# Readers of one PSUM buffer in another order: a decoder layer's cross attention and its FiLM step

## The chip, the cores and the metric

The kernel runs on one core of a Trainium2 chip. A core has five engines with a queue of instructions each: TensorE (PE in the profile: matmuls, and PEld for the loads of their stationary operand), VectorE (DVE), ScalarE (ACT), GpSimd (POOL) and SyncE (SP, which issues DMAs here). They run beside each other and are ordered among each other by semaphores alone. The metric is the device time of one execution in microseconds (us); less is better.

## The reference

The computation is a two-layer decoder on x of 16 sequences x 256 rows x 256 columns, with a context of 77 rows x 192 columns for each sequence. Layer 0 is windowed attention, cross attention and a network of eight experts. Layer 1 is what the change lies in; cut to it, on x after layer 0:

```python
x = x + _L1_attn_ref(_layernorm(x))      # RWKV: a scan over the 16 sequences, then a channel mix
# _L1_xattn_ref(x_text = _layernorm(x), x_vision = ctx_768):
Q, K = x_text @ Wq, x_vision @ Wk                            # 4 heads of 32
topv, topi = jax.lax.top_k(scores, K_TOP)                    # the 32 best of 77 keys
attn_mean = attn.mean(axis=1)                                # mean over the heads
c_t = einsum(attn_mean, x_vision @ Wv)
x = layernorm(x_text, g_norm_in, b_norm_in)
scale_in, shift_in = split(c_t @ W_film_in + b_film_in)
x = x * (1.0 + mod_gate * scale_in) + mod_gate * shift_in    # FiLM before the state space model
y = s4d(x, ...)                                              # a filter, by a Fourier transform
scale_out, shift_out = split(c_t @ W_film_out + b_film_out)
y = y * (1.0 + mod_gate * scale_out) + mod_gate * shift_out  # FiLM behind it
xt = x_text + y
h = layernorm(xt, g_ffn, b_ffn); xt = xt + gelu(h @ W1 + b1) @ W2 + b2
return layernorm(xt, g_norm_out, b_norm_out)
# then x = x + _L1_ffn_ref(_layernorm(x)): a product with a sign matrix, scaled and clipped
```

## The kernel before

The first half of the program (to about 915 us) is layer 0; the change doesn't touch it. The second half is one function, `mixing_and_state_space`, a software pipeline over the 16 sequences. Its loop has 20 steps, n = 0 to 19, and each engine's queue is written out by hand: every engine runs the same loop and calls its own pieces in its own order. In step n the pieces of five sequences are at work: t = n is in the RWKV scan, c = n - 1 in its channel mix and at the head of the cross attention, j = n - 2 in the top-k and FiLM, i = n - 3 in the filter and the gelu network, p = n - 4 in the last norm and the output. A step in which all five are there is called full (n = 4 to 15). There is no scheduler; what stands first in a queue is issued first, and an instruction whose wait is not met holds all behind it on its engine.

The places that the change touches, by step:

- The mean attention `am` (VectorE, `average`, L1765) is turned on TensorE (`turn_average`, L2269) into the PSUM buffer `p_T`, and ScalarE copies it out to `amT` (`average`, L2052). The buffer `p_T` is used by all transposes, so whatever is turned next waits until ScalarE has read what is in it. This is what `latest(pe, (e["amT"], n - 2), ...)` in `turn_E` says: it takes the first pair of its list that exists and waits for that one.
- `turn_E` (TensorE, L2159, operand `E_hE`) turns the normed rows of the next sequence into `p_T`; ScalarE copies them (`turned`, L2029, to `hT`), and `queries_keys` (L2241 to L2244) multiplies them into queries and keys.
- `network` (TensorE, L2326) is the second product of the gelu network: 8 blocks for each of two row tiles a = 0, 1. One block is one 128x256 product, which the profile counts as two MATMUL records.
- `film` (TensorE, L2279) multiplies `amT` with the folded FiLM weights for row tile t = 0 and then t = 1, 1024 columns each, into the two banks of the PSUM buffer `p_S`. Bank 0 holds scale_in and shift_in, bank 1 scale_out and shift_out. The bank pair is used again for t = 1, so `film` of tile 1 waits until tile 0 has been read.
- The readers of `p_S`: VectorE `film` (L1771, L1773: `u` times scale_in, plus shift_in; L1775: `hE` plus shift_out) and ScalarE `film` (L2057: copies scale_out to `fo`).
- `exps_E` (ScalarE, L2041: the exponentials of the scores, 8 instructions) and `turned_3` (ScalarE, L2067: the transposed rows of the gelu network's input out of `p_T`, counted in `n3T`, which the first product `hidden(i, 0)` on TensorE, L2316, waits for).

`scores` (TensorE, L2251) writes `p_S` anew for the next sequence, so it waits for the readers of tile 1 as well. `inverse` (L2297) is the last product of the filter; VectorE's `scale_out` (L1794) reads its result.

Of the kernel before, what the change touches and what calls it, by code (L numbers as in the profile page):

```python
# [1364 lines left out]
def mixing_and_state_space(nc, args, k, place, ys_dram, cxT, cxU, out, ahead, lw, folded_film, folded_row, spectrum_in):  # L1365
# [6 lines left out]
    with ExitStack() as ctx:  # L1372
# [226 lines left out]
        def _(dve):  # L1599
# [3 lines left out]
            def chained(instruction):  # L1603
                nonlocal steps
                steps += 1
                instruction.then_inc(step["dve"], 1)
# [160 lines left out]
            def film(j, t):  # L1767
                if t == 0:
                    dve.wait_ge(e["n1"], j + 1)
                dve.wait_ge(e[f"fp{t}"], j + 1)  # L1770
                chained(v.tensor_tensor(u[:, t, :], u[:, t, :], p_S[:, 0, 0:D], ALU.mult))  # L1771
                settled()
                v.tensor_tensor(u[:, t, :], u[:, t, :], p_S[:, 0, D:2 * D], ALU.add).then_inc(e["u"], 1)  # L1773
                dve.wait_ge(e[f"fo{t}"], j + 1)
                v.tensor_tensor(hE[:, j % 2, t, :], hE[:, j % 2, t, :], p_S[:, 1, D:2 * D], ALU.add).then_inc(e["hs"], 1)  # L1775

            def spectrum(i):
                dve.wait_ge(e["Up"], i + 1)
# [126 lines left out]
        def _(act):  # L1905
# [148 lines left out]
            def film(j, t):  # L2054
                past(act, e["xb"], j - 1)
                act.wait_ge(e[f"fp{t}"], j + 1)
                a_.activation(fo[:, t, :], p_S[:, 1, 0:D], ACT.Copy).then_inc(e[f"fo{t}"], 1)  # L2057

            def n_3(i):
# [31 lines left out]
            for n in range(B + 4):  # L2091
                t, c, j, i, p = n, n - 1, n - 2, n - 3, n - 4
                if t < B:
                    fall_4(t)
                if 0 <= c < B:
                    channel_mixes_A(c)
                if t < B:
                    values(t)
                    gates(t)
                    falls(t)  # L2100
                if 0 <= c < B:
                    channel_mixes_B(c)
                    gate_channel(c)
                if 0 <= p < B:
                    h_6(p)
                if 0 <= c < B:
                    rectify(c, 0, 0)
                    rectify(c, 0, 1)
                if t + 1 < B:
                    h_1(t + 1)  # L2110
                if 0 <= p < B:
                    turned(f["T6"], f["h6T"], p)
                if t < B:
                    exps_D(t)
                if t + 1 < B:
                    n_1(t + 1)
                if 0 <= c < B:
                    square(c, 0)
                    rectify(c, 1, 0)
                    rectify(c, 1, 1)  # L2120
                    square(c, 1)
                if t + 1 < B:
                    mixes_A(t + 1)
                    mixes_B(t + 1)
                if 0 <= i < B:
                    n_3(i)
                if 0 <= j < B:
                    context(j)
                if 0 <= i < B:
                    turned_3(i)  # L2130
                if 0 <= j < B:
                    exps_E(j)
                    n_E(j)
                if 0 <= i < B:
                    gelu(i, 0)
                    gelu(i, 1)
                if 0 <= c < B:
                    h_E(c)
                if 0 <= j < B:
                    average(j)  # L2140
                if t < B:
                    n_2(t)
                if 0 <= c < B:
                    turned(e["Th"], e["hT"], c)
                if 0 <= j < B:
                    film(j, 0)
                if 0 <= c < B:
                    queries(c)
                if 0 <= j < B:
                    film(j, 1)  # L2150

        @block.tensor
        def _(pe):
# [92 lines left out]
            def scores(j):  # L2246
                pe.wait_ge(e["qT"], j + 1)
                pe.wait_ge(e["kTz"], j + 1)
                past(pe, e["hs"], 2 * j - 1)
                for t in range(2):  # L2250
                    last = te.matmul(p_S[:, t, 0:H * J], qkT[:, t * P:(t + 1) * P], kTz[:].rearrange("p h j -> p (h j)"),  # L2251
                                     start=True, stop=True)
                last.then_inc(e["scp"], 1)
# [18 lines left out]
            def film(j, t):  # L2272
                if t == 0:
                    pe.wait_ge(e["amT"], j + 1)
                    pe.wait_ge(e["vw"], j + 1)
                else:
                    pe.wait_ge(e["hs"], 2 * j + 1)
                for q in range(2):
                    last = te.matmul(p_S[:, q, :], amT[:, t * P:(t + 1) * P], w["VW"][:, q * 512:(q + 1) * 512],  # L2279
                                     start=True, stop=True)  # L2280
                last.then_inc(e[f"fp{t}"], 1)
# [61 lines left out]
            for n in range(B + 4):  # L2343
# [50 lines left out]
                    network(n, i, 1, 0, FB // 2)  # L2394
                if 0 <= j < B:
                    turn_average(n, j)
                if 0 <= i < B:
                    network(n, i, 1, FB // 2, FB)
                if 0 <= c < B:
                    turn_E(n, c)  # L2400
                if 0 <= j < B:
                    film(j, 0)
                if 0 <= c < B:
# [74 lines left out]
```

## Time and profile before

| | us |
|---|---|
| median of 3 runs (1896.68 to 1900.81) | 1900.28 |
| the profiled execution's own time | 1900.81 |
| its span in the profile | 1899.1 |
| TensorE busy | 1632.9 (86%) |
| VectorE busy | 1312.9 (69%) |
| ScalarE busy | 866.0 (46%) |
| GpSimd busy | 655.4 (35%) |
| mean granted clock of TensorE | 0.933 of full speed |

A row of a timeline has the start in us from the span's beginning, the time in us to the end of the last of the merged instructions, the engine, the line, the operation, output<-inputs, and how many instructions are merged (x8). In square brackets stands how long the engine sat idle before the row and whose result ended that. Instructions of one engine overlap a little at their ends, so the next row can start before the sum of start and time; TensorE's ends are modelled. The busy share of TensorE over the whole span says little about the loop, since layer 0 and the ends of the loop have other limits; the loop is read from its own stretch. The granted clock is 1.00 (2.4 GHz) or 0.50 (1.2 GHz) at each moment.

### The profile page before, as it was taken

What the parts mean: (1) busy time and instruction counts of PE and PEld (TensorE: products, weight loads), DVE (VectorE), ACT (ScalarE), POOL (GpSimd) and SP (SyncE); (2) the same over time, 40 slices, a digit from 0 to 9 for tenths busy, and PEclk for the clock granted to TensorE, in tenths of its full rate; (3) what the DMA queues carried; (4) which work ended last, traced back from release to release, by engine and by line L of the source; (5) the groups of instructions that cost most, each with busy time, mean ns of one, the idle gap of its engine ahead of it and who ended that gap; (6) DMA issues with size and microseconds to landing.
All of it is one profiled execution on the core that took longest, in us unless ns stands there. A gap on an engine that the chain in (4) does not pass through costs nothing.

```text
span 1899.1 us, 26400 instructions
## 1 busy us (share of the span) xinstructions
PE 1632.9 (86%) x7946; PEld 1260.9 (66%) x7946; DVE 1312.9 (69%) x4214; ACT 866.0 (46%) x1714; POOL 655.4 (35%) x1016
## 2 busy tenths in 40 slices
PE   5899999993199999993677999999999999998775
PEld 3677777772066766772555777777778777776544
DVE  2467777764047777542567899898889899987642
ACT  1344444441022111113555666777766667754331
POOL 1122222212500000004444566556556555543221
PEclk9899999996599999997788999999999999999876
DMA  8000000004844343435000000000000000000000
GB/s 261 19 1 1 1 1 1 1 1 154 327 129 137 100 118 98 129 114 191 6 6 6 7 12 12 7 12 12 12 6 12 12 6 7 7 6 7 0 6 11
DMA packets 81060, 92.91 MB, mean 49 GB/s; under 512 B 19142, under 2 KB 69527, under 8 KB 80667
## 3 DMA queue, kind: packets, MB, share of 16 engines
q1 hardware_dynamic: 72235, 77.73, 12.8%
q0 software_dynamic: 3072, 8.39, 1.3%
q10 hardware_dynamic: 5616, 5.11, 0.8%
q8 instruction: 67, 1.10, 0.2%
q14 instruction: 70, 0.57, 0.1%
HBM read 70.76 MB, written 20.45 MB: 48 GB/s over the span
## 4 chain that ended last, share of the span: by engine, by line
PE 26%; DVE 20%; issue 3%; ACT 2%; POOL 2%; DMA 0%; POOLq 0%; DVEq 0%; ACTq 0%
PE E_pK L2218 5%; PE E_pK L2177 3%; PE E_pS L2279 3%; DVE E_wk L1748 3%; DVE E_ex L1680 2%; PE E_pY L2326 2%; PE E_pY L2165 2%; PE E_pY L2297 2%; DVE E_m L1741 2%; PE E_pU L2288 1%; DVE E_st L1613 1%; PE E_pY L2177 1%; PE E_pT L2159 1%; PE E_pY L2228 1%; PE E_pU L2316 1%
## 5 line engine op out<-in xcount | busy, mean ns | idle before, releaser
L1226 ACT ACTIVATE F_uT<-F_puT 128x512 f32<-128x512 f32 x78 | 42.8, 595 | 287.5 <-PE F_puT L1287 256.5
L1277 PE MATMUL F_pu<-C_W,F_hT 128*128 x312 | 145.3, 610 | 1.2 <-issue 1.2
L1498 POOL TENSOR_SCALAR E_var<-E_mv 128x2 f32<-128x2 f32 x80 | 42.1, 527 | 292.9 <-DVE E_mv L1617 291.8
L1297 PE MATMUL F_py<-C_W,F_uT 128*128 x624 | 141.3, 380 | 0.5 <-ACT F_uT L1226 0.5
L2316 PE MATMUL E_pU<-E_xT,E_W 128*128 128x256 f32 x512 | 121.5, 393 | 7.2 <-ACT E_hid L2075 4.9
L1297 PEld LDWEIGHTS F_py<-C_W,F_uT 128*128 128x128 f32 x624 | 115.9, 191 | 15.0 <-issue 1.2
L2228 PE MATMUL E_pY<-E_Wcv,E_hid 128*128 128x256 f32 x512 | 119.6, 389 | 4.0 <-issue 2.4
L2228 PEld LDWEIGHTS E_pY<-E_Wcv,E_hid 128*128 128x128 f32 x512 | 97.2, 195 | 28.9 <-issue 16.7
L2316 PEld LDWEIGHTS E_pU<-E_xT,E_W 128*128 128x128 f32 x512 | 101.1, 198 | 22.9 <-ACT E_hid L2075 5.7
L2326 PE MATMUL E_pY<-E_W,E_hid 128*128 128x256 f32 x512 | 115.6, 380 | 0.0
L2218 PE MATMUL E_pK<-E_cmix,E_Wck 128*128 128x256 f32 x512 | 115.3, 380 | 0.0
L989 POOL TENSOR_SCALAR F_var<-F_mv 128x1 f32<-128x1 f32 x39 | 8.6, 222 | 302.6 <-DVE F_mv L1001 302.6
L2218 PEld LDWEIGHTS E_pK<-E_cmix,E_Wck 128*128 128x128 f32 x512 | 96.5, 191 | 12.3
L2326 PEld LDWEIGHTS E_pY<-E_W,E_hid 128*128 128x128 f32 x512 | 96.4, 191 | 12.2
L222 POOL TENSOR_SCALAR A_varB<-A_mvB 128x2 f32<-128x2 f32 x16 | 3.5, 217 | 280.1 <-DVE A_mvB L261 280.1
L1277 PEld LDWEIGHTS F_pu<-C_W,F_hT 128*128 128x128 f32 x312 | 58.2, 197 | 61.2 <-issue 61.2
L1020 DVE TENSOR_TENSOR F_u<-F_pu,F_b 128x512 f32<-128x512 f32 x78 | 52.1, 689 | 42.9 <-PE F_pu L1277 42.7
L1748 DVE MATCH_REPLACE8 E_wk<-E_m,E_wk 128x77 f32<-128x77 f32 x384 | 80.6, 224 | 0.0
L2075 ACT ACTIVATE E_hid<-E_pU,b 128x256 f32<-128x256 f32 x128 | 52.0, 472 | 51.7 <-PE E_pU L2316 51.5
L2177 PE MATMUL E_pK<-E_mix,Wkvr 128*128 128x256 f32 x256 | 65.1, 401 | 9.4 <-DVE E_mix L1650 9.4
L581 PE MATMUL A_pqa<-A_hTB,A_Wq 128*128 128x256 f32 x256 | 66.4, 407 | 5.1 <-ACT A_hTB L430 5.1
L999 DVE BATCH_NORM_STATS2 F_st<-F_xs 128x6 f32<-128x256 f32 x39 | 16.6, 426 | 75.4 <-DMA F_xs<-sorted_x 74.9
(408 smaller groups left out, 4295.4 us busy)
## 6 DMA issues: line engine op xcount, KB each, us to landing
F_b<-in_L_ffn_b SPq DMA_DIRECT2D x39, 512.0 KB, 4.3
C_W<-in_L_ffn_W SPq DMA_DIRECT2D x16, 1024.0 KB, 13.9
sorted_x<-zero SPq DMA_DIRECT2D x1, 4992.0 KB, 19.6
F_xs<-sorted_x SPq DMA_DIRECT2D x39, 128.0 KB, 2.3
F_b<-in_L_ffn_b SPq DMA_DIRECT2D x39, 128.0 KB, 3.1
sorted_y<-F_y ACTq DMA_DIRECT2D x39, 128.0 KB, 2.2
out<-E_tB SPq DMA_DIRECT2D x16, 256.0 KB, 2.1
X<-in_x SPq DMA_DIRECT2D x3, 1024.0 KB, 10.7
```

Source lines behind the costliest of these rows:

```text
L581: last = te.matmul(p_qa[:, half, (m % 2) * S:(m % 2 + 1) * S], Wq[:, kb, m * P:(m + 1) * P], hTB[:, kb, :], start=kb == 0, stop=kb == KD - 1)
L1020: ve.tensor_tensor(u[:, cols], p_u[:, f, :], b1[:, i % 2, cols], ALU.add).then_inc(s[f"u{f}"], 1)
L1277: last = nc.tensor.matmul(p_u[:, f, :], hT[:, i % 2, kb, :], W1[:, bass.ds(e, 1), kb, f * 512:(f + 1) * 512], start=kb == 0, stop=kb == KD ...
L1297: last = nc.tensor.matmul(p_y[:, 0:D], uT[:, f, :], W2[:, bass.ds(e, 1), f, :], start=f == 0, stop=f == FB - 1)
L1748: last = v.match_replace(wk[:, t, hd, :], m8[:, turn, t, hd, :], src[:, t, hd, :], TAKEN)
L2075: last = a_.activation(hid[:, fb, :], p_U[:, q, :], ACT.Gelu, bias=b1[:, fb:fb + 1])
L2177: last = te.matmul(to[:, o, :], Wkvr[:, m, kb, o * P:(o + 1) * P], mix[:, m, kb, :], start=kb == 0, stop=kb == KD - 1)
L2218: last = te.matmul(p_K[:, q, :], Wck[:, kb, fb * P:(fb + 1) * P], cmix[:, 0, kb, :], start=kb == 0, stop=kb == KD - 1)
L2228: last = te.matmul(p_Y[:, a, :], hid[:, fb, a * P:(a + 1) * P], Wcv[:, fb, :], start=fb == 0, stop=fb == FB - 1)
L2279: last = te.matmul(p_S[:, q, :], amT[:, t * P:(t + 1) * P], w["VW"][:, q * 512:(q + 1) * 512], start=True, stop=True)
L2316: last = te.matmul(p_U[:, q, :], W1[:, kb, fb * P:(fb + 1) * P], xT[:, kb, :], start=kb == 0, stop=kb == KD - 1)
L2326: last = te.matmul(p_Y[:, a, :], hid[:, fb, a * P:(a + 1) * P], W2[:, fb, :], start=fb == 0, stop=fb == FB - 1)
```

## The change

Four edits, all in `mixing_and_state_space`:

1. VectorE `film`: the sum into `hE` stands between the product and the sum into `u`, and it no longer waits for ScalarE's copy.
2. ScalarE `film`: the copy of scale_out now waits until VectorE has finished the sum into `u` of the same tile (which, since VectorE's queue is in order, is behind the sum into `hE`). Both who write `p_S` next (`film` of tile 1, `scores`) wait for `u` and for ScalarE's copy, where they waited for `hs`.
3. ScalarE: `exps_E` stands ahead of `turned_3`.
4. TensorE: `turn_E` stands ahead of the second half of `network` for row tile 1, right behind `turn_average`.

```diff
@@ VectorE, film(j, t)
                 chained(v.tensor_tensor(u[:, t, :], u[:, t, :], p_S[:, 0, 0:D], ALU.mult))
+                v.tensor_tensor(hE[:, j % 2, t, :], hE[:, j % 2, t, :], p_S[:, 1, D:2 * D], ALU.add).then_inc(e["hs"], 1)
                 settled()
                 v.tensor_tensor(u[:, t, :], u[:, t, :], p_S[:, 0, D:2 * D], ALU.add).then_inc(e["u"], 1)
-                dve.wait_ge(e[f"fo{t}"], j + 1)
-                v.tensor_tensor(hE[:, j % 2, t, :], hE[:, j % 2, t, :], p_S[:, 1, D:2 * D], ALU.add).then_inc(e["hs"], 1)
@@ ScalarE, film(j, t)
                 act.wait_ge(e[f"fp{t}"], j + 1)
+                act.wait_ge(e["u"], 2 * j + 1 + t)
                 a_.activation(fo[:, t, :], p_S[:, 1, 0:D], ACT.Copy).then_inc(e[f"fo{t}"], 1)
@@ ScalarE, the loop
                 if 0 <= j < B:
                     context(j)
+                    exps_E(j)
                 if 0 <= i < B:
                     turned_3(i)
                 if 0 <= j < B:
-                    exps_E(j)
                     n_E(j)
@@ TensorE, scores(j)
-                past(pe, e["hs"], 2 * j - 1)
+                past(pe, e["u"], 2 * j - 1)
+                past(pe, e["fo1"], j - 1)
@@ TensorE, film(j, 1)
-                    pe.wait_ge(e["hs"], 2 * j + 1)
+                    pe.wait_ge(e["u"], 2 * j + 1)
+                    pe.wait_ge(e["fo0"], j + 1)
@@ TensorE, the loop
                 if 0 <= j < B:
                     turn_average(n, j)
+                if 0 <= c < B:
+                    turn_E(n, c)
                 if 0 <= i < B:
                     network(n, i, 1, FB // 2, FB)
-                if 0 <= c < B:
-                    turn_E(n, c)
```

TensorE's queue in a full step, before, from the end of `network` for tile 0 to the first product of the next step (x4 here is four 128x256 products, the profile's x8):

```order
 L2326 MATMUL E_pY<-E_W,E_hid 128x256 x12
 L2269 MATMUL E_pT<-ident,E_am 77x128 x2
 L2326 MATMUL E_pY<-E_W,E_hid 128x256 x4
 L2159 MATMUL E_pT<-ident,E_hE 128x128 x4
 L2279 MATMUL E_pS<-E_VW,E_amT 128x512 x2
```

The same place after the change:

```order
 L2328 MATMUL E_pY<-E_W,E_hid 128x256 x12
 L2270 MATMUL E_pT<-ident,E_am 77x128 x2
 L2159 MATMUL E_pT<-ident,E_hE 128x128 x4
 L2328 MATMUL E_pY<-E_W,E_hid 128x256 x4
 L2281 MATMUL E_pS<-E_VW,E_amT 128x512 x2
```

The four products that stood between the two writers of `p_T` now stand behind the second one.

ScalarE's queue in a full step, before, from the input norm of the gelu network to its first gelu:

```order
 L1919 ACTIVATE E_n<-E_fo,E_nmr,E_rs 128x256 x2
 L2046 ACTIVATE E_VW<-E_pS 77x1024
 L2067 ACTIVATE E_xT<-E_pT,bf,gf 128x256 x2
 L2041 ACTIVATE E_ex<-E_sc,E_nmx 128x77 x8
 L1925 ACTIVATE E_u<-E_hE,E_rs2E 128x256 x2
```

The same place after the change:

```order
 L1918 ACTIVATE E_n<-E_fo,E_nmr,E_rs 128x256 x2
 L2045 ACTIVATE E_VW<-E_pS 77x1024
 L2040 ACTIVATE E_ex<-E_sc,E_nmx 128x77 x8
 L2067 ACTIVATE E_xT<-E_pT,bf,gf 128x256 x2
 L1924 ACTIVATE E_u<-E_hE,E_rs2E 128x256 x2
```

The eight exponentials stand ahead of the two copies out of `p_T` for which TensorE waits.

## Rows read from the trace of the kernel before

**Rows 1.** Stretches: length, each engine's busy us (instructions), granted clock, DMA share, GB/s.
```profile
1062.83:1720.79 657.96, 640.29 (x2901) 513.40 (x2901) 592.86 (x1988) 458.13 (x932) 377.52 (x538) 1.00 0.03 9
1728.00:1738.00 10.00, 6.20 (x29) 4.62 (x28) 9.18 (x22) 4.38 (x10) 3.07 (x8) 1.00 0.00 1
```

**Rows 2.** Chain that ended last, 1290 to 1420 us: start, us, engine, output, line.
```profile
1309.04 0.70 DVE E_fo L1794
...
1335.72 1.20 DVE E_am L1765
...
1363.89 0.70 DVE E_fo L1794
```

**Rows 3.** Timeline of TensorE, 1300 to 1365 us, around the turn.
```profile
1322.21 3.62 PE L2316 MATMUL E_pU<-E_xT,E_W 128*128 128x256 f32 x16
1325.66 1.89 PE L2165 MATMUL E_pY<-E_Wo,E_num 128*128 128x256 f32 x8
...
1336.97 0.44 PE L2269 MATMUL E_pT<-ident,E_am 128*77 128x128 f32 x2 [0.79 <-DVE E_am L1765]
1337.25 1.89 PE L2326 MATMUL E_pY<-E_W,E_hid 128*128 128x256 f32 x8
1338.98 0.60 PE L2159 MATMUL E_pT<-ident,E_hE 128*128 128x128 f32 x4
1339.41 1.88 PE L2279 MATMUL E_pS<-E_VW,E_amT 78*128 78x512 f32 x4
...
1342.67 1.98 PE L2279 MATMUL E_pS<-E_VW,E_amT 78*128 78x512 f32 x4
...
1364.38 0.66 PE L2159 MATMUL E_pT<-ident,E_n1D 128*128 128x128 f32 x4 [0.53 <-ACT E_n1D L1925]
```

**Rows 4.** Timeline of ScalarE, 1300 to 1365 us.
```profile
1320.68 1.02 ACT L2067 ACTIVATE E_xT<-E_pT,bf,gf 128x256 f32<-128x256 f32 x2 [0.81 <-PE E_pT L2159]
1321.59 2.10 ACT L2041 ACTIVATE E_ex<-E_sc,E_nmx 128x77 f32<-128x77 f32 x8
...
1337.45 0.38 ACT L2052 ACTIVATE E_amT<-E_pT 77x256 f32<-77x256 f32 x1 [4.59 <-PE E_pT L2269]
...
1341.39 0.38 ACT L2057 ACTIVATE E_fo<-E_pS 128x256 f32<-128x256 f32 x1 [1.18 <-PE E_pS L2279]
...
1363.44 0.89 ACT L1925 ACTIVATE E_n1D<-E_hD,E_rs2D 128x256 f32<-128x256 f32 x2
```

**Rows 5.** Timeline of VectorE, 1300 to 1365 us.
```profile
1328.10 0.68 DVE L1694 SCALAR_TENSOR_TENSOR E_x<-E_pY,E_hD 128x512 f32<-128x512 f32 x1
...
1341.40 0.42 DVE L1771 TENSOR_TENSOR E_u<-E_u,E_pS 128x256 f32<-128x256 f32 x1 [1.90 <-PE E_pS L2279]
1341.86 0.42 DVE L1773 TENSOR_TENSOR E_u<-E_u,E_pS 128x256 f32<-128x256 f32 x1
1342.20 0.41 DVE L1775 TENSOR_TENSOR E_hE<-E_hE,E_pS 128x256 f32<-128x256 f32 x1
```

**Rows 6.** Timeline of TensorE in step 2, where no network stands behind the turn.
```profile
1007.46 0.71 PE L2269 MATMUL E_pT<-ident,E_am 128*77 128x128 f32 x2 [11.36 <-DVE E_am L1765]
1008.74 1.09 PE L2159 MATMUL E_pT<-ident,E_hE 128*128 128x128 f32 x4 [0.56 <-ACT E_amT L2052]
```

**Rows 7.** Timelines of steps 16 and 17, engines mixed, in order of time.
```profile
1758.21 1.02 ACT L2067 ACTIVATE E_xT<-E_pT,bf,gf 128x256 f32<-128x256 f32 x2 [4.58 <-PE E_pT L2159]
...
1765.65 5.38 PE L2316 MATMUL E_pU<-E_xT,E_W 128*128 128x256 f32 x16 [2.30 <-ACT E_hid L2075]
1771.33 1.21 DVE L1765 TENSOR_REDUCE E_am<-E_ex 128x154 f32<-128x616 f32 x1
1776.04 0.38 PE L2269 MATMUL E_pT<-ident,E_am 128*77 128x128 f32 x2
...
1810.70 1.28 ACT L2041 ACT_TABLE_LOAD   x1
1810.73 3.72 PE L2316 MATMUL E_pU<-E_xT,E_W 128*128 128x256 f32 x16 [1.15 <-ACT E_xT L2067]
```

## The prediction, made before the changed kernel ran

> **What bounds the kernel now.** I read three views, in this order. First the stretches: from the turn of `am` in step 3 to that in step 15 lie 657.96 us, twelve periods of 54.83 us at full clock [rows 1]. So each microsecond added to a period counts twelve times, and TensorE, though busy 640.29 / 12 = 53.36 us of each, is idle 1.4 us in it.
>
> Then the chain of waits, which says what closes the period. It runs as a ring: VectorE takes the filter's result at 1309.04 (L1794), works without a wait to the end of `am` at 1335.72 + 1.20 = 1336.92, then the chain is on TensorE until `inverse` gives the next filter result to VectorE at 1363.89 [rows 2]. One round is 54.85 us: 27.9 on VectorE and 27.0 on TensorE. The reader is to see that TensorE's idle time lies outside the second part: it waits 0.79 us for `am`, and 0.53 us behind `inverse` [rows 3]. Both waits sit beside VectorE's part of the ring. Time added to TensorE between `turn_average` and `inverse` is therefore not taken up by them; time added to TensorE between `inverse` and `turn_average` is, up to 0.79 us, unless VectorE itself waits for the delayed product.
>
> Last the timelines at the edited places, for the price of each wait.
>
> **Edit 4, `turn_E` right behind `turn_average`.** Both write `p_T`, so `turn_E` needs ScalarE's copy `amT`. Before, the four products of `network` (1337.25 to 1338.98) lay over that copy. Now TensorE stands still. Count from the start of `turn_average` [rows 3, 4]: the copy starts 1337.45 - 1336.97 = 0.48 later and takes 0.38; from a ScalarE result to TensorE's start it is 1364.38 - (1363.44 + 0.89) = 0.05. So `turn_E` starts at +0.91, where the next instruction started at +0.28 before: 0.63 idle. The same row of `n1D` shows that four transposes behind such a wait take 0.66 instead of 0.60, so `film(0)` comes at 0.63 + 0.07 = 0.70 us later. Step 2 already has this order, with no `network` in between, and shows the wait: 0.56 us [rows 6], at half clock. Bounds: that 0.56, and 0.80 by the whole of step 2's hand-over (1008.74 - 1007.46 - 0.71 = 0.57, from the end of the one to the start of the other, where I have 0.47). I take 0.70, since it is built from the rows of a full step. What is queued behind the wait is TensorE's whole ring part. The gain that could stand against it, an earlier copy of `hE` to `hT`, is worth nothing: before, `queries_keys` started straight behind `film(0)` without a wait. It happens in steps 3 to 16.
>
> **Edits 1 and 2, the readers of `p_S`.** From `film(0)`'s start at 1339.41, VectorE starts at +1.99 (1341.40), and `film(1)` starts at +3.26 (1342.67), just behind the end of the sum into `hE` (1342.61) [rows 3, 5]. After: product at +1.99; the sum into `hE` needs nothing from it and follows in 0.34 (the distance of the last two rows of rows 5), the sum into `u` again 0.34 behind and takes 0.42: +3.09. VectorE gains 0.1 us a tile. But only then does ScalarE copy, which before ran beside it (1341.39 beside 1341.40): start +3.14, end +3.52, `film(1)` at +3.57. That is 0.31 us later. Bounds: 0.18 (the copy's 0.38 less 0.2 if all overlaps are perfect) and 0.52 (each hand-over 0.1 slower). I take 0.31.
>
> The Trainium skill ("VectorE: DVE Perf Modes", section "The DRAIN you can't avoid") says that a next VectorE operation does not start until the pipe of the one before is empty, so that order and semaphores change nothing. This trace disagrees: behind a dependence the next start is 0.46 us on (1341.40 to 1341.86), without one 0.34 (to 1342.20) [rows 5]. By the rule the three would take 1.34 instead of 1.10 us, and the sum would be 12 x 0.24 = 2.9 us higher.
>
> Tile 1 is not on the path in full steps: its readers run behind VectorE's `add_network`, long before `scores` and `forward`. `qkT` moves by some 0.1 us, and `kTz` has slack.
>
> **Edit 3, `exps_E` ahead of `turned_3`.** ScalarE sat idle 0.81 us before `turned_3`, from 1319.87 [rows 4]. Now the exponentials start there, and take 1321.59 to 1321.59 + 2.00 before what follows starts, so `turned_3` starts at about 1321.8 and ends at 1322.8. TensorE's `hidden(0)` started at 1322.21 [rows 3] and now starts at 1322.8 to 1322.9: 0.6 to 0.7 later. Then `out_product` ends at 1325.66 + 1.89 + 0.65 = 1328.20, where VectorE wanted its result at 1328.10 [rows 5]. VectorE's ring part grows by about 0.10 us (bounds 0 and 0.20), and the rest of the 0.65 is taken up by the wait for `am`. The gelus start 0.8 us sooner, but in full steps TensorE doesn't wait for them. It counts in steps 4 to 14, eleven times. In steps 15 and 16 ScalarE idles over 4 us before `turned_3` for want of the turn (4.58 in step 16 [rows 7]), so the exponentials fit in.
>
> **The sum.** Ring: 12 x (0.70 + 0.31) = 12.1; 11 x 0.10 = 1.1; `film(1)` of step 2, 0.3. Together 13.5 us.
>
> The last steps are another case [rows 7]. Step 15: 0.70 + 0.1 (VectorE's `kTz`, and not `film(1)`, is on the path there) = 0.8. Step 16: the exponentials fill the idle 4.58 us before 1758.21, so the gelus come about 2.4 us sooner and `hidden(1)`'s wait of 2.30 us goes, and with it the half clock behind it (5.38 us instead of the 3.62 of rows 3). `network` would be 4.2 us earlier, but `am` ends at 1771.33 + 1.21 = 1772.54 and now `turn_average` waits for it: 1772.6 instead of 1776.04, a gain of 3.4. Then 0.70 and 0.34 are lost again. Step 17: `turned_3` stood ahead of the exponentials and their table load without a wait, `hidden(0)` started at 1810.73; it now starts 1.28 + 2.0 = 3.3 us later, but `hidden(1)` no longer waits for the gelus: +0.5. `film(1)` +0.31, and there `forward` follows straight on `u`, which is done 0.23 later since another sum stands before it. Together 0.8 - 3.4 + 1.0 + 1.0 = -0.6.
>
> In all +12.9 us on the profiled execution's 1900.8 (span 1899.1 and 1.7 around it), so 1913.7. It stands 0.5 above the median of the runs; against the median I say 1913.2.
>
> **The rivals.**
> - A: the ring is not where I put it, and the new waits fit in the 1.32 us that TensorE idles per step. Then the loop stays at 54.83 us and only the ends move, -0.6 - 0.8 = about 1899. If VectorE's shorter `film` (0.2 us a step) then even shortens the period, 12 x 0.2 = 2.4 come off as well: 1896.5, faster. For it: 1.32 is more than 1.01. Against it: VectorE has no wait between 1309.04 and 1336.92, and none of those idle pieces lies in TensorE's part of the ring. It decides from the period: at 54.8 or below this holds. 8% (5% of them faster).
> - B: the clock falls. For it: in step 16 a wait of 2.30 us was followed by products at half clock, at a price of 5.38 - 3.62 = 1.76 us [rows 7]; after the change 0.2 to 0.7 + 0.63 + 0.3 us of idle lie within 6 us. Against it: between 1728 and 1738 TensorE was idle 3.8 of 10 us and the granted clock stayed 1.00 [rows 1]. If it fell in each of the twelve periods: 12 x 1.76 = 21 more, 1934. 6%. The Trainium skill ("TensorE: Matmul & The Clock Gate", section "A second HAM failure mode: psum-queue depth-cycling") has a kernel in which short idle pieces between groups of matmuls were enough to make the clock swing; by it this rival would be the likely one, and in this trace the stretch from 1728 speaks against it.
> - C: edit 3 costs its full delay, since VectorE has less slack at L1694 than its row shows. Then each period is 0.5 longer: 1919. 7%.
> - D: edit 4 costs nothing (the copy to `amT` is done when `turn_E` comes). Then 14 x 0.70 go: 1903.4. Step 2 speaks against it. 4%.
>
> **How the numbers follow.** My own sum has 75%. With the low bounds it is 12 x 0.74 + 0.3 - 0.6 - 1.5 (a better end of step 17) = +7, with the high ones 12 x 1.32 + 11 x 0.2 + 0.3 - 0.6 + 1.5 = +19. The range of 1906 to 1921 leaves out A, B and D and thin ends of my own. Within 0.2% of before (3.8 us, about what a measurement of this kernel can tell from no change) lie part of A and D: 5%. Faster 5%, slower 90%.
>
> **What would show it.** In the profile after: the period from `turn_average` to `turn_average` at 55.9 us instead of 54.83; a wait of about 0.6 us before L2159 (`E_hE`) for `amT` in 15 steps; one of about 0.3 us before L2281 for `fo`; L2318 waiting about 0.6 us for `xT`, and the wait for `am` shrunk to 0.2 to 0.3; in step 16 no wait for a gelu; clock 1.00 through the full steps. A period of 54.8 would refute the ring, one above 57 would mean the clock or a wait that I did not see.

## The result and the profile after

| | before | after |
|---|---|---|
| median of the timed runs, us | 1900.55 (1896.68 to 1905.17, 4 runs) | 1920.62 (1919.13 to 1922.87, 4 runs) |
| profiled execution, us | 1900.81, span 1899.1 | 1922.16, span 1920.5 |
| period of a full step, us | 54.83 | 56.22 to 56.25 |
| mean granted clock | 0.933 | 0.931 |

The ratio is 1.0104, with a 95% interval of 1.009 to 1.0118: slower, as predicted, by 20 us where 12.9 were forecast. 1920.6 lies just inside the predicted range (1906 to 1921), 0.4 us below its upper end; the profiled execution's 1922.2 lies above it.

First the stretch from the turn of `am` in step 3 to that in step 15, whose counterpart is [rows 1] (columns as there). The second row is a part of step 17, with a mean granted clock of 0.66: the last steps run partly at half clock, which the loop never does.

```profile
1063.56:1738.25 674.69, 645.64 (x2901) 511.68 (x2901) 591.26 (x1988) 455.94 (x932) 377.76 (x538) 1.00 0.03 9
1800.00:1830.00 30.00, 17.56 (x44) 10.97 (x44) 21.51 (x95) 5.36 (x8) 11.46 (x18) 0.66 0.03 10
```

The loop became 674.69 - 657.96 = 16.7 us longer at full clock, with the same 2901 matmuls: the time is in waits. Of the 21.3 us between the two profiled executions this is 16.7; 0.7 came before step 3's turn (1063.56 against 1062.83), and behind step 15's turn lie 1920.5 - 1738.25 = 182.3 us where before there were 1899.1 - 1720.79 = 178.3: another 3.9.

One period of TensorE, with [rows 3] as its counterpart (timeline: start, us, engine, line, operation, idle time before the row and what ended it):

```profile
1330.43 3.72 PE L2318 MATMUL E_pU<-E_xT,E_W 128*128 128x256 f32 x16 [0.48 <-ACT E_xT L2067]
1333.98 1.89 PE L2165 MATMUL E_pY<-E_Wo,E_num 128*128 128x256 f32 x8
...
1344.78 0.45 PE L2270 MATMUL E_pT<-ident,E_am 128*77 128x128 f32 x2 [0.28 <-DVE E_am L1765]
1345.79 0.63 PE L2159 MATMUL E_pT<-ident,E_hE 128*128 128x128 f32 x4 [0.56 <-ACT E_amT L2051]
1346.25 1.89 PE L2328 MATMUL E_pY<-E_W,E_hid 128*128 128x256 f32 x8
1347.98 1.88 PE L2281 MATMUL E_pS<-E_VW,E_amT 78*128 78x512 f32 x4
1351.70 1.96 PE L2281 MATMUL E_pS<-E_VW,E_amT 78*128 78x512 f32 x4 [0.42 <-ACT E_fo L2057]
...
1373.38 0.66 PE L2159 MATMUL E_pT<-ident,E_n1D 128*128 128x128 f32 x4 [0.54 <-ACT E_n1D L1924]
```

Three new waits stand where the prediction put them: 0.56 before `turn_E`, 0.42 before `film(1)`, 0.48 before `hidden(0)`. The wait for `am` shrank from 0.79 to 0.28. `film(0)` comes 1347.98 - 1344.78 = 3.20 behind `turn_average` (before 2.44), and `film(1)` 3.72 behind `film(0)` (before 3.26).

The same places in the chain of waits (start, us, engine, output, line), which now runs through the added waits:

```profile
1343.54 1.20 DVE E_am L1765
1344.74 0.04 issue
1344.78 0.46 PE E_pT L2270 x2
1345.26 0.39 ACT E_amT L2051
1345.65 0.14 issue
1345.79 0.63 PE E_pT L2159 x4
...
1351.17 0.39 ACT E_fo L2057
1351.56 0.14 issue
1351.70 1.96 PE E_pS L2281 x4
```

The reader is to see the two pieces of 0.14 named "issue": the hand-over from ScalarE's copy to a TensorE that stands waiting. From the end of `am` on VectorE to TensorE it is 0.04.

ScalarE and VectorE at the edited places, against [rows 4] and [rows 5]:

```profile
1327.34 2.13 ACT L2040 ACTIVATE E_ex<-E_sc,E_nmx 128x77 f32<-128x77 f32 x8
1329.34 1.04 ACT L2067 ACTIVATE E_xT<-E_pT,bf,gf 128x256 f32<-128x256 f32 x2
...
1345.26 0.38 ACT L2051 ACTIVATE E_amT<-E_pT 77x256 f32<-77x256 f32 x1 [4.08 <-PE E_pT L2270]
...
1351.17 0.38 ACT L2057 ACTIVATE E_fo<-E_pS 128x256 f32<-128x256 f32 x1 [4.06 <-DVE E_u L1774]
```

```profile
1335.91 0.69 DVE L1694 SCALAR_TENSOR_TENSOR E_x<-E_pY,E_hD 128x512 f32<-128x512 f32 x1 [0.15 <-PE E_pY L2165]
...
1349.97 0.42 DVE L1771 TENSOR_TENSOR E_u<-E_u,E_pS 128x256 f32<-128x256 f32 x1 [2.65 <-PE E_pS L2281]
1350.31 0.42 DVE L1772 TENSOR_TENSOR E_hE<-E_hE,E_pS 128x256 f32<-128x256 f32 x1
1350.64 0.41 DVE L1774 TENSOR_TENSOR E_u<-E_u,E_pS 128x256 f32<-128x256 f32 x1
```

VectorE's three instructions of a tile now follow at 0.34 and 0.33 and end at 1351.05 (+3.07 behind `film(0)`, predicted +3.09). ScalarE starts 0.12 later, and `film(1)` 0.15 behind the copy's end. VectorE, which before had no wait between L1794 and `am`, now has one of 0.15 at L1694.

### The profile page after: what moved, and what is told of

It reads as the page before. It is cut to its first block, busy times and chain, and to the rows that moved or that the text cites. A ratio compares the mean times of both kernels' runs of the same rounds, so it can differ in the third digit from the quotient of the medians.

```text
span 1920.5 us, 26433 instructions
## 1 busy us (share of the span) xinstructions
PE 1642.0 (85%) x7946; PEld 1260.9 (66%) x7946; DVE 1310.4 (68%) x4214; ACT 864.1 (45%) x1714; POOL 655.7 (34%) x1016
## 4 chain that ended last, share of the span: by engine, by line
PE 25%; DVE 12%; ACT 11%; issue 4%; POOL 2%; DMA 0%; ACTq 0%; DVEq 0%; POOLq 0%
PE E_pK L2177 3%; PE E_pU L2318 3%; PE E_pY L2165 3%; PE E_pK L2218 3%; PE E_pS L2281 3%; PE E_pY L2328 2%; DVE E_wk L1748 2%; ACT E_mixB L1930 2%; PE E_pU L2290 1%; PE E_pY L2177 1%; ACT E_mix L1930 1%; ACT E_ex L2040 1%; PE E_pY L2228 1%; PE E_pT L2159 1%; DVE E_m L1741 1%
## 5 line engine op out<-in xcount | busy, mean ns | idle before, releaser
L2281 PE MATMUL E_pS<-E_VW,E_amT 78*128 78x512 f32 x128 | 64.9, 631 | 7.7 <-ACT E_fo L2057 7.7
## 6 DMA issues: line engine op xcount, KB each, us to landing
X<-in_x SPq DMA_DIRECT2D x3, 1024.0 KB, 10.6
```

## The experiments

The theory under test: the full step is a ring, 27.9 us on VectorE and 27.0 us on TensorE; an edit costs what it adds to one of the two parts; the price of edit 4 is uncovered copy time, that of edits 1 and 2 the copy behind three VectorE instructions, that of edit 3 the part of `hidden(0)`'s delay that exceeds VectorE's slack. The rivals: the waits are taken up by TensorE's idle time; the granted clock; or one edit alone is to blame. Periods below are the mean of the twelve from step 3's turn to step 15's, in the profile. The kernel before had medians of 1900.55, 1904.1 and 1899.53 in the three sets of runs, so only ratios within a set are compared.

### Each edit alone

**Edit 4 alone.**

```diff
                     turn_average(n, j)
+                if 0 <= c < B:
+                    turn_E(n, c)
                 if 0 <= i < B:
                     network(n, i, 1, FB // 2, FB)
-                if 0 <= c < B:
-                    turn_E(n, c)
```

> Only edit 4: turn_E right behind turn_average, everything else as before. My theory: TensorE's part of the ring is on the path, so the step from turn_average to the next turn_average grows by the idle time in front of turn_E. The profile after has +0.76 us there (film(0) at +3.20 behind turn_average, before +2.44): period 55.6 us, 12 x 0.76 = 9.1 us on the loop, total about +10 (14 steps). Rival A (TensorE's idle time takes it up): period 54.8, total +1 or less. Rival 'the edits are worth more together': period below 55.3. The tail: if step 17's extra 4.3 us of the profile after comes from here, the total is +13 or more.

Measured: ratio 1.0068 (1.0048 to 1.0089), about 12.9 us (9 to 17 by the interval). Period (1733.77 - 1067.05) / 12 = 55.56, that is +0.73, or 8.8 us over the twelve. The rest is not located. It isn't in step 17, where the expectation looked for it: the profile has turn 16 to turn 17 at 50.21 us (before 51.33).

```profile
1344.84 0.44 PE L2269 MATMUL E_pT<-ident,E_am 128*77 128x128 f32 x2 [0.76 <-DVE E_am L1765]
1345.84 0.63 PE L2159 MATMUL E_pT<-ident,E_hE 128*128 128x128 f32 x4 [0.56 <-ACT E_amT L2052]
1346.30 1.89 PE L2326 MATMUL E_pY<-E_W,E_hid 128*128 128x256 f32 x8
1348.03 1.88 PE L2279 MATMUL E_pS<-E_VW,E_amT 78*128 78x512 f32 x4
```

TensorE still waits 0.76 us for `am` here, as before, and yet the period is longer: idle time in VectorE's part of the ring doesn't pay for idle time in TensorE's part. Rival A falls. This is the largest single price.

**Edits 1 and 2 alone.**

```diff
                 chained(v.tensor_tensor(u[:, t, :], u[:, t, :], p_S[:, 0, 0:D], ALU.mult))
+                v.tensor_tensor(hE[...], hE[...], p_S[:, 1, D:2 * D], ALU.add).then_inc(e["hs"], 1)
                 settled()
                 v.tensor_tensor(u[...], u[...], p_S[:, 0, D:2 * D], ALU.add).then_inc(e["u"], 1)
-                dve.wait_ge(e[f"fo{t}"], j + 1)
-                v.tensor_tensor(hE[...], hE[...], p_S[:, 1, D:2 * D], ALU.add).then_inc(e["hs"], 1)
...
+                act.wait_ge(e["u"], 2 * j + 1 + t)
                 a_.activation(fo[:, t, :], p_S[:, 1, 0:D], ACT.Copy).then_inc(e[f"fo{t}"], 1)
```

The waits of `scores` and of `film` of tile 1 on TensorE are those of the change.

> Only edits 1 and 2 (order of VectorE's sums, ScalarE's copy behind the sum into u). My theory: film(1) comes 0.46 us later behind film(0) (+3.72 instead of +3.26), all of it on the path: period 55.3 us, total about +6. As I had predicted it: +0.31, period 55.1, total about +4. Rival 'hidden': period 54.8, total within 1 us of before.

Measured: ratio 1.0039 (1.0023 to 1.0056), about 7.4 us (4.4 to 10.6). Period (1723.67 - 1060.81) / 12 = 55.24, +0.41, or 4.9 us over the twelve.

```profile
1339.42 1.88 PE L2281 MATMUL E_pS<-E_VW,E_amT 78*128 78x512 f32 x4
...
1343.14 1.96 PE L2281 MATMUL E_pS<-E_VW,E_amT 78*128 78x512 f32 x4 [0.42 <-ACT E_fo L2057]
```

`film(1)` stands at +3.72, the value of the kernel after.

**Edit 3 alone.**

```diff
                     context(j)
+                    exps_E(j)
                 if 0 <= i < B:
                     turned_3(i)
                 if 0 <= j < B:
-                    exps_E(j)
                     n_E(j)
```

> Only edit 3 (exponentials ahead of turned_3). My theory: hidden(0) starts 0.6 us later, VectorE's part grows by 0.1 to 0.2, the rest is taken up in TensorE's wait for am: period 54.9 to 55.0, +2 us on the loop; step 16 3.4 us shorter. What is open is step 17: if the exponentials with their table load ahead of turned_3 cost there what the profile after has (hidden(0) waits 4.86 us), the ends come to about +1 and the total is +1 to +3; if that came from another edit, the total is near -1. Rival C (its full delay on the path): period 55.4, total +7.

Measured: ratio 0.9991 (0.9976 to 1.0007), no difference that the runs can tell. Period (1722.11 - 1060.76) / 12 = 55.11, +0.28 (0.07 to 0.17 expected), so 3.4 us lost in the loop; behind step 15's turn 1897.2 - 1722.11 = 175.1 us, 3.2 less than before. The step from turn 15 to turn 16 took 51.78 us (before 55.25), the next 53.36 (before 51.33). One period, first TensorE, then VectorE:

```profile
1432.49 2.86 PE L2316 MATMUL E_pU<-E_xT,E_W 128*128 128x256 f32 x12 [0.53 <-ACT E_xT L2067]
...
1436.05 1.89 PE L2165 MATMUL E_pY<-E_Wo,E_num 128*128 128x256 f32 x8
```

```profile
1437.97 0.69 DVE L1694 SCALAR_TENSOR_TENSOR E_x<-E_pY,E_hD 128x512 f32<-128x512 f32 x1 [0.22 <-PE E_pY L2165]
```

From `hidden(0)` to `out_product` it is 3.56 us (before 3.45, [rows 3]): a group of products behind a wait takes 0.11 us longer until the next one starts. `hidden(0)` is 0.69 later in its period, `out_product` thus 0.80, and L1694, which before had 0.55 to spare, starts 0.29 later (0.25 beyond the slack, and 0.03 of hand-over).

The three periods add up: 0.73 + 0.41 + 0.28 = 1.42, and the whole change has 674.69 / 12 - 54.83 = 1.39 over twelve periods and 1.42 in eleven of them. The edits don't interact in a full step.

### What the price of an edit is made of

**`turn_E` with two products of cover.**

```diff
                     turn_average(n, j)
                 if 0 <= i < B:
-                    network(n, i, 1, FB // 2, FB)
+                    network(n, i, 1, FB // 2, FB // 2 + 2)
                 if 0 <= c < B:
                     turn_E(n, c)
+                if 0 <= i < B:
+                    network(n, i, 1, FB // 2 + 2, FB)
```

> As before, but with turn_E two products earlier: turn_average, two products of network, turn_E, the other two. My theory (the price of edit 4 is idle time before turn_E that those products covered): turn_E can start at about +1.0 behind turn_average, two products end at +1.14, so nothing is uncovered: period 54.8, total within 1 us of before. Rival (the price lies in turn_E standing ahead of the rest of network, whatever covers the copy: the later ffp, or the copy to hT that cannot be used earlier): period 55.2 to 55.6, total +5 to +10.

Measured: period (1720.58 - 1062.84) / 12 = 54.81; ratio 1.0011 (0.9994 to 1.0028).

```profile
1336.87 0.44 PE L2269 MATMUL E_pT<-ident,E_am 128*77 128x128 f32 x2 [0.76 <-DVE E_am L1765]
1337.15 1.03 PE L2326 MATMUL E_pY<-E_W,E_hid 128*128 128x256 f32 x4
1338.02 0.60 PE L2159 MATMUL E_pT<-ident,E_hE 128*128 128x128 f32 x4
```

The two products (x4, as four are x8 in [rows 3]) cover 1338.02 - 1337.15 = 0.87 us, and the wait is gone. So it is the missing cover that costs, not the earlier place of `turn_E`.

**The copy beside the sum into `u`.** Against edits 1 and 2 alone:

```diff
                 act.wait_ge(e[f"fp{t}"], j + 1)
-                act.wait_ge(e["u"], 2 * j + 1 + t)
+                act.wait_ge(e["hs"], 2 * j + 1 + t)
```

> Edits 1 and 2 with one difference: ScalarE's copy waits for the sum into hE instead of the sum into u, so that it runs beside the sum into u (they read different banks). My theory (the price of edits 1 and 2 is the copy behind all three VectorE instructions): film(1) waits for the copy or the sum into u, whichever is later; the copy ends 0.3 us earlier than in the kernel after, so film(1) comes at about +3.40 instead of +3.72 behind film(0), before +3.26: period 54.95 us, total about +1.5. Rival (the price comes from waiting for two semaphores or from VectorE's new order): film(1) stays at +3.7, period 55.2, total +6.

Measured: `film(1)` at 1349.80 - 1346.41 = +3.39, period (1728.42 - 1069.37) / 12 = 54.92, as expected; ratio 0.9981 (0.9963 to 0.9999). In the loop it costs 1.1 us, yet the runs come out 0.2% under before, by an interval that barely leaves out no difference. In the profile the stretch behind step 15's turn is 1904.1 - 1728.42 = 175.7 us, 2.6 less than before. Of this 1.7 is clock: the sixteen products behind the wait for the gelus in step 16, which this edit doesn't touch, ran at full clock (3.72 us, before 5.38 [rows 7]). The rest is open. The order on VectorE is cheap; the copy behind the third instruction is what costs 0.3 us a step.

```profile
1349.80 1.96 PE L2281 MATMUL E_pS<-E_VW,E_amT 78*128 78x512 f32 x4
```

### Using the ring the other way

**Two products of `network` ahead of `turn_average`**, none of the four edits:

```diff
-                    network(n, i, 1, 0, FB // 2)
+                    network(n, i, 1, 0, FB // 2 + 2)
                 if 0 <= j < B:
                     turn_average(n, j)
                 if 0 <= i < B:
-                    network(n, i, 1, FB // 2, FB)
+                    network(n, i, 1, FB // 2 + 2, FB)
```

> Neither of the four edits; instead two of the four products of network that stand behind turn_average go ahead of it, into the 0.79 us in which TensorE waits for am. My theory (a ring of 27.9 us on VectorE and 27.0 us on TensorE between turn_average and inverse; only what lies in a part counts): TensorE's part becomes 27.0 - 0.87 = 26.1, the period 54.0 us, the wait for am goes to under 0.1 us, turn_E stays covered by the two products left: 12 x 0.85 = 10 us less, about 1890. Rival (the order on TensorE doesn't matter as long as it does the same work, i.e. the ring is not there): period 54.8, same time. Rival (the two products ahead delay turn_average by their whole 0.87 us): period 54.8 too, with turn_average later behind am.

Measured: ratio 0.9924 (0.9899 to 0.9949), 14 us faster than before (10 to 19 by the interval). Period (1713.55 - 1066.02) / 12 = 53.96, where 54.0 was expected. The loop is 657.96 - 647.53 = 10.4 us shorter; what lies above that is not located.

```profile
1335.83 0.44 PE L2269 MATMUL E_pT<-ident,E_am 128*77 128x128 f32 x2
1336.11 1.03 PE L2326 MATMUL E_pY<-E_W,E_hid 128*128 128x256 f32 x4
1336.98 0.60 PE L2159 MATMUL E_pT<-ident,E_hE 128*128 128x128 f32 x4
1337.42 1.88 PE L2279 MATMUL E_pS<-E_VW,E_amT 78*128 78x512 f32 x4
```

The profile shows no wait before `turn_average` any more, but it still starts 0.05 behind the end of `am` (1334.59 + 1.19 on VectorE): the ring still closes there. And `film(0)` follows it at +1.59 instead of +2.44. The work is the same and every product still runs; two of them moved from the part of the ring that counts into a wait that did not. This is the strongest evidence for the ring.

**The same done to the kernel after.**

> The kernel after, with two products of network ahead of turn_average instead of behind turn_E. Done to the kernel before, this took 0.87 us off each period, since TensorE had 0.79 us of waiting for am to fill. The kernel after waits only 0.28 us for am. My theory (the period is the longer of two: the ring, and TensorE's own work with the waits that nothing can fill): the ring would be 56.25 - 0.87 = 55.38, but TensorE's own sum is 56.25 - 0.28 = 55.97, so the period is 55.97, the wait for am is gone, and the total is only 3 to 4 us less than after. Rival (the ring alone decides): 55.4, total 10 us less.

Measured: ratio 1.0048 (1.003 to 1.0066) against before, where the kernel after has 1.0104. That is 10.6 us less than after, the rival's number and not the 3 to 4 of my theory; but the two ratios are of different sets of runs, and of the 10.6 only 674.69 - 668.14 = 6.6 lie in the twelve periods. The periods decide. The turns of steps 3 and 15 stand at 1059.09 and 1727.23; eleven of the twelve periods are 55.73 or 55.74, the last 55.06.

```profile
1387.46 6.21 PE L2328 MATMUL E_pY<-E_W,E_hid 128*128 128x256 f32 x28
1393.51 0.38 PE L2270 MATMUL E_pT<-ident,E_am 128*77 128x128 f32 x2
1394.45 0.63 PE L2159 MATMUL E_pT<-ident,E_hE 128*128 128x128 f32 x4 [0.56 <-ACT E_amT L2051]
```

Only 0.51 us of the 0.87 came back: the ring through VectorE alone (55.4) is refuted as the bound here. `am` now ends 0.47 us before `turn_average` starts (1336.11 + 1.19 on VectorE, 1337.77), so VectorE's part of the ring is off the path. The profile's chain of waits closes over ScalarE instead: it goes over from TensorE at about 1415, stays on ScalarE to the end of `turned_3` at 1434.4, whose result `hidden(0)` waits for, and runs on TensorE from there to the turn. My 55.97 was 0.24 too high, since a wait costs more than the idle time printed for it. From the start of the last group of `network` to the turn it is 1393.51 - 1387.46 = 6.05 us for 28 records without a wait, so 6.05 - 0.87 = 5.18 for 24; in the kernel after it is 1401.04 - 1395.42 = 5.62 for 24 with the wait of 0.28. That wait cost 0.44. And `turn_E` starts 0.94 instead of 1.01 behind the turn. 56.25 - 0.44 - 0.07 = 55.74, the period measured.

### The last steps

**Edit 3 in steps 15 and 16 alone**, on the kernel before:

```diff
+                if 0 <= j < B and (j >= B - 3 and j < B - 1):
+                    exps_E(j)
                 if 0 <= i < B:
                     turned_3(i)
                 if 0 <= j < B:
-                    exps_E(j)
+                    if not (j >= B - 3 and j < B - 1):
+                        exps_E(j)
```

> The kernel before with edit 3 in steps 15 and 16 alone. The profiles had the step from turn_average 15 to turn_average 16 3.5 us shorter with edit 3; the timed medians of the kernels with two products ahead, with and without it, did not differ. If the 3.5 us are real for each execution: period 54.83 in the full steps, 51.7 in step 16, total 3.5 us under before, ratio 0.998. If they were the granted clock of those executions: ratio 1.000.

Measured: ratio 0.9983 (0.9969 to 0.9997), about 3.2 us; full periods 54.80 to 54.83.

```profile
1740.83 3.64 PE L2168 MATMUL E_pY<-E_Wcr,E_cmix 128*128 128x256 f32 x8 [2.27 <-DVE E_cmix L1702]
...
1766.53 7.07 PE L2319 MATMUL E_pU<-E_xT,E_W 128*128 128x256 f32 x32
...
1779.38 0.44 PE L2272 MATMUL E_pT<-ident,E_am 128*77 128x128 f32 x2 [0.59 <-DVE E_am L1765]
```

Both halves of `hidden` run through in step 16, without the wait of 2.30 and the half clock of [rows 7], and `turn_average` waits 0.59 for `am`: what the prediction said of step 16. But the step from turn 15 to turn 16 took 53.48 us where 51.7 was expected, since the eight products of the first row ran at half clock (before, behind the same wait: 2.00). The next step gave that back (49.62 us, before 51.33), since there the sixteen products behind the gelus' wait of 2.65 ran at full clock (3.72, before 5.25). Together it is 3.5 us, and the interval leaves out no difference: there is a gain, and how much of it is the edit's own and how much the clock's, one profile doesn't tell.

**The half clock of the last steps comes and goes.** The wait of [rows 7] for the gelus in step 16 (2.29 to 2.32 us) stands in six of the kernels. Behind it the sixteen products took 5.38, 5.29 and 5.39 us in three (before, edit 4 alone, two products ahead) and 3.72 in the other three, here with edits 1 and 2 alone:

```profile
1768.65 3.72 PE L2318 MATMUL E_pU<-E_xT,E_W 128*128 128x256 f32 x16 [2.29 <-ACT E_hid L2075]
```

In step 17, behind 2.65 to 2.67 us, they took 5.19 to 5.35 us in four kernels and 3.72 in five. So of the 3.5 us that edit 3 gains in step 16, some 1.7 are there only against an execution in which this group runs at half clock.

**Both gains together.** The two products ahead and this form of edit 3:

> The kernel above, with edit 3 in steps 15 and 16 alone, where the run with edit 3 alone had the step from turn to turn 3.5 us shorter, and not in the full steps, where it cost 0.28 us each, nor in step 17, where it cost 2.0. My theory: 3.5 to 5 us less than the kernel above, about 1886. Rival (a shorter step 16 only shifts the wait into step 17, as the granted clock falls there): within 1 us of the kernel above.

Measured: ratio 0.9918 (0.9889 to 0.9946). It is the fastest by its ratio, but does not differ measurably from 0.9924 (medians 1888.15 and 1887.70), which is the rival's number; the profile has the step from turn 15 to turn 16 at 52.72 us against 56.96 without edit 3, and the next one unchanged (51.29 and 51.33), which is not the rival's reason. Whether the 3 us arrive in every execution is not settled by six and nine runs.

**Step 17.** The kernel after, with edit 3 taken back in that step alone (`exps_E` ahead of `turned_3` only for `j < B - 1`):

> The kernel after, with edit 3 taken back in step 17 alone. The kernel after lost 3.9 us behind turn_average of step 15, where I had predicted a gain of 0.6. Theory X (edit 3 in step 17: hidden(0) waits 4.9 us for the table load and the exponentials, at half clock behind it): hidden(0) waits about 1.2 us again, and 2 to 4 us come back, total 1917. Theory Y (the loss is the granted clock of the last steps, set by where TensorE happens to stand idle, and not by edit 3): within 1 us of the kernel after, 1920, with the stretch behind step 15 still at 182 us.

In the kernel after, step 17 looks like this, ScalarE first, then TensorE:

```profile
1828.83 1.28 ACT L2040 ACT_TABLE_LOAD   x1
1830.12 2.10 ACT L2040 ACTIVATE E_ex<-E_sc,E_nmx 128x77 f32<-128x77 f32 x8
1832.13 1.00 ACT L2067 ACTIVATE E_xT<-E_pT,bf,gf 128x256 f32<-128x256 f32 x2
```

```profile
1833.18 9.88 PE L2318 MATMUL E_pU<-E_xT,E_W 128*128 128x256 f32 x32 [4.86 <-ACT E_xT L2067]
```

And with edit 3 taken back there:

```profile
1834.63 3.72 PE L2321 MATMUL E_pU<-E_xT,E_W 128*128 128x256 f32 x16 [1.44 <-ACT E_xT L2067]
1840.99 3.72 PE L2321 MATMUL E_pU<-E_xT,E_W 128*128 128x256 f32 x16 [2.65 <-ACT E_hid L2075]
```

The step from turn 16 to turn 17 took 53.96 us instead of 57.17, and from step 15's turn to the end it was 1922.0 - 1743.10 = 178.9 instead of 182.3. In that profile theory X holds: the table load and the exponentials before `turned_3` cost 3.2 us in step 17. By the rows: the products start 4.86 - 1.44 = 3.4 later, and from there to `network` it is 9.72 us against 9.92, as the half clock in the thirty-two products (9.88 instead of the 7.07 of step 16 above) costs about what the missing wait of 2.65 gives; together 3.2. The times do not settle it: 1.0087 (1.0059 to 1.0116) against 1.0104 for the whole change is a difference of 3.2 us, but the intervals overlap, and the median of 1921.1 is not the 1917 expected. Its profiled execution had lost 4.8 us before step 3's turn instead (1068.36 against 1063.56).

## Why the prediction came out as it did

- **The total: inside the range, in part by luck.** It came out 7.4 us above the 1913.2 forecast and 0.4 below the range's end. Of the 8.4 us that the profiled execution lies above its forecast, 3.5 are the loop, 4.5 the steps behind step 15's turn and 0.4 the time ahead of step 3's. The upper bound had 18.0 for the twelve periods, which took 16.7, but only 0.9 for the last steps, which took 3.9. Rival C's 1919 was nearer to the total than my sum; only the period rules it out.
- **The ring, and that nothing in it is free: right.** (TensorE's idle time in a period is 54.83 - 53.36 = 1.47 us, where the prediction says 1.4; nothing rests on it.) Each edit alone lengthens the period, with the wait for `am` still there (edit 4); and work moved out of TensorE's part shortens it by what the ring says (53.96 against 54.0).
- **Edit 4, +0.70: right, measured 0.76 at `film(0)` and 0.73 in the period** (`turn_E` at +1.00, said +0.91). Both lie between my value and the upper bound from step 2's row (0.80). The hand-over from ScalarE was 0.14 and not the 0.05 of the `n1D` row.
- **Edits 1 and 2, +0.31: the mechanism right, the size too small, measured 0.46 at `film(1)` and 0.41 in the period.** VectorE's three instructions ended within 0.02 us of the forecast: 0.34 and 0.33 from start to start where each takes 0.42, against the 0.46 before for a sum that waits for the product just ahead of it. The prediction set this against the Trainium skill ("VectorE: DVE Perf Modes", section "The DRAIN you can't avoid"), but gave only a part of it: the section also says that a next instruction which isn't held starts earlier. The trace agrees with that, and disagrees with its remark that leaving semaphores out gains nothing. What was missing are the hand-overs: 0.12 to ScalarE instead of 0.05, 0.15 to TensorE instead of 0.05. My bound of 0.52 ("each hand-over 0.1 slower") held it.
- **Edit 3, +0.10 in the ring: the mechanism right, the size wrong by a factor of three, measured 0.28**, above my bound of 0.20. The step that failed is "`out_product` ends at 1325.66 + 1.89 + 0.65": `hidden(0)` came 0.69 later, and 0.11 more went where the products start again behind a wait. A part was arithmetic: the prediction's own rows give 1319.87 + 2.00 + 1.02 + 0.05 = 1322.94, so 0.73 later and not 0.65. Of a delay that is nearly covered, an error of 0.15 is more than the cost itself.
- **The ring's sum:** 16.7 us instead of 13.2. The miss is 12 x (0.03 + 0.10) + 11 x 0.18 = 3.5, most of it in hand-overs that I had taken from one other row (`n1D`'s 0.05) and in the restart behind a wait, which I had left out for `hidden(0)`.
- **Step 16, a gain of 3.4 less the 0.8 of step 15: right, in part by luck.** The step from turn 15 to turn 16 took 52.66 us instead of 55.25, 2.6 less; no wait for a gelu. But 1.76 of the 3.4 is the half clock of [rows 7], which comes and goes: the step took 53.72 us with edits 1 and 2 alone, where it should have grown, and 57.61 with edit 4 alone, where a second group ran at half clock (3.13 us for the eight products that took 2.00 before).
- **Step 17, +0.5 for edit 3: wrong.** Said: 3.3 us later at `hidden(0)`, but then no wait for the gelus. Both happened, but the products behind a wait of 4.9 us began at half clock. Alone, edit 3 lengthened that step by 2.0 us, in the kernel after by 3.2. My "-0.6" for all behind step 15's turn was +3.9 in the profile. Laid beside the rows of before, the 4.5 us of this miss are: `hidden(0)` comes 42.27 us behind turn 16 instead of 34.69, 7.6 later where 4.3 were said. 3.4 of that is the table load and the exponentials, as forecast; 1.8 is clock, in the row below, which took 1.97 before; 2.4 lie earlier in the step, where 1.0 was said and `forward` ran slower too (3.62 us, before 2.97). From `hidden(0)` to `network` 1.7 us came back, where 2.8 were said.

```profile
1821.10 3.75 PE L2165 MATMUL E_pY<-E_sign,E_xT 128*128 128x256 f32 x8 [0.88 <-DVE E_fo L1793]
```

The term that failed here is one that the prediction left out: it takes the products of step 17 at the clock that they had before. Why they ran slower stays open.

- **Rival A (absorbed)** falls with edit 4 alone. **Rival B (the clock falls in each period)** falls: 1.00 over the twelve periods in every profile. The Trainium skill ("TensorE: Matmul & The Clock Gate", section "A second HAM failure mode: psum-queue depth-cycling") tells of a kernel whose clock swung with short idle pieces between groups of matmuls; these periods, with waits of 0.48, 0.28, 0.56, 0.42 and 0.54 us, show no such swing. **Rival C (edit 3 at full delay, 0.5)** falls with 0.28; **rival D (edit 4 free)** with 0.73.

**What stays open.** The last steps and the start of the loop differ between profiles of kernels that are the same there: step 3's turn stood between 1059.09 and 1069.37, with the first period 55.4 or 55.8 us in three kernels and 59.1 to 59.3 in the others. The clock goes with it. Here the stretch from 1014 to 1020, at the end of step 2 and the start of step 3, of the kernel before, and then of the one with two products of `network` ahead, which has no `network` so early and so the same instructions there:

```profile
1014.00:1020.00 6.00, 6.00 (x26) 4.40 (x25) 4.37 (x11) 0.99 (x3) 1.19 (x2) 0.94 0.16 44
```

```profile
1014.00:1020.00 6.00, 6.00 (x12) 3.39 (x12) 2.83 (x8) 0.83 (x2) 0.93 (x1) 0.50 0.14 44
```

Nearly full clock in the one (0.94), half in the other, and this makes up the difference between their first periods (55.37 and 59.14 us): the transposes `E_n` at the start of step 3 already stand 11.46 us behind step 2's turn in the one and 15.23 in the other. One profile of a kernel therefore can't tell a few us at the ends. What sets off the half clock, why the early copy came out faster than before in the rest, and what part of the tail's 3.9 us belongs to the change, would take several profiles of each.

## What to carry to other kernels

Find the ring that closes the period, and split it by engine: a wait in the other engine's part is not slack for this engine's part, but it is a place where this engine's work can go (two products moved there took 0.87 us off each period, 10.4 us in the loop, where the four edits cost 16.7). Where a reorder puts a consumer right behind its producer through another engine's copy, price the start, the copy and both hand-overs, and take each hand-over from a row where the receiving engine is really standing. An edit whose delay just about fits into a slack should be carried with its whole delay as the upper bound, and an edit that helps in the drain and hurts in the full steps can be given by step number.

## What the runs showed of the hardware that was not expected

- From the end of ScalarE's single copy to a waiting TensorE it took 0.14 to 0.15 us (`amT`, `fo`, in four kernels), but 0.04 to 0.06 behind `turned_3` and `n1D`, which are two instructions each. From VectorE to TensorE (`am`) it was 0.04, from VectorE to ScalarE (`u`) 0.12. Why the two ScalarE cases differ wasn't tried.
- Sixteen products behind a wait took 3.56 us until the next group instead of 3.45. And a wait costs more than the idle time printed before its row, which is counted from the modelled end of the row before: 0.28 printed were 0.44 in the distance of the starts (5.62 against 5.18).
- Behind a TensorE wait of 4.6 to 4.9 us in step 17 the next products ran slowly (32 in 9.88 us instead of 7.07); sixteen behind one of 1.44 ran at full clock (3.72). Behind waits of 2.3 and of 2.65 us the same sixteen took 5.2 to 5.4 us in some kernels and 3.72 in others, and eight behind one of 2.27 took 2.00 or 2.9 to 3.7: the length of the wait alone doesn't say which.
